# Routed results reach X by accumulating DMAs from POOL instead of loads and POOL adds

## What is computed

```python
x = x + 0.5 * _L0_ffn_ref(_layernorm(x), ...)
x = x + _L0_attn_ref(_layernorm(x), ...)
x = x + 0.5 * _L0_ffn_ref(_layernorm(x), ...)
# _L0_ffn_ref: 0.5 * shared experts + 0.5 * (each token's two best of 8 experts, weighted)
# _L0_attn_ref, per sequence of 256 tokens:
#   q, k, v = split(rms_norm(x) @ w_qkv); q, k = rms_norm(q), rms_norm(k); w = exp(k)
#   y = sigmoid(q) * cumsum(w * v) / (cumsum(w) + 1e-6)
#   u, g = split(y @ w_swiglu); x + (u * silu(g)) @ w_out
```

## Time and profile before

| what | value |
|---|---|
| runs (us) | 766.91, 769.57, 769.66; median 769.57 |
| profiled execution (us) | 770.35; its span, first to last instruction, 768.6 |
| busy share of the span | PE 89%, DVE 59%, POOL 54%, ACT 44% |
| chain that ended last | PE 68%, DVE 20%, ACT 3%, issue 3%, POOL 2%, DMA 2% |
| first add of results on POOL | 335.59 us |
| last write of attention to X | 455.46 us |
| DMA issued by POOL | 284, all indirect; 18.78 MB on its queue |

### The profile page before, as it was taken

The page is one execution under the profiler, slowest core; times in us unless marked ns, Lnnn a source line. Parts: engine busy times, 40 slices in busy tenths (PEclk is TensorE's granted clock), DMA queues, the critical chain, the costliest instruction groups (busy, mean ns, idle before and its releaser), DMA issues.

```text
span 768.6 us, 12871 instructions
## 1 busy us (share of the span) xinstructions
PE 686.6 (89%) x4282; PEld 583.7 (76%) x4282; DVE 453.1 (59%) x1137; ACT 336.7 (44%) x833; POOL 418.4 (54%) x491
## 2 busy tenths in 40 slices
PE   3879849999999999976887777999999999999995
PEld 3667738888888888953664575788888888888883
DVE  6678874444444444447999986884444444444435
ACT  2658412444444444416664526662444444444430
POOL 5600484476676665369997515006367666765330
PEclk9989959999999999999999997999999999999999
DMA  9450011111121111031100000502011112112037
GB/s 311 192 96 16 2 24 34 32 49 46 46 53 46 46 46 42 22 114 54 43 29 1 1 1 24 89 1 50 22 50 49 46 46 52 46 46 42 29 105 247
DMA packets 34782, 43.97 MB, mean 57 GB/s; under 512 B 5984, under 2 KB 27488, under 8 KB 34336
## 3 DMA queue, kind: packets, MB, share of 16 engines
q1 hardware_dynamic: 25632, 24.39, 11.2%
q0 software_dynamic: 9088, 18.78, 9.6%
HBM read 27.47 MB, written 15.66 MB: 56 GB/s over the span
## 4 chain that ended last, share of the span: by engine, by line
PE 68%; DVE 20%; ACT 3%; issue 3%; POOL 2%; DMA 2%; SPq 1%; POOLq 0%; DVEq 0%; ACTq 0%
PE psY L1466 16%; PE psH L1449 8%; PE psG L1307 6%; PE psU L1307 5%; PE psU L1309 5%; PE psG L1309 5%; PE psU L1308 5%; PE psG L1308 5%; PE psH L1378 5%; DVE rec L1063 3%; PE psT L1406 2%; DVE XN L736 2%; DVE hs L746 2%; DVE ln_stats L723 1%; DVE xn L1047 1%
## 5 line engine op out<-in xcount | busy, mean ns | idle before, releaser
L942 DVE SCALAR_TENSOR_TENSOR hr<-silu,gate,psU 128x512 f32<-128x512 f32 x142 | 106.2, 748 | 165.4 <-PE psU L1309 165.4
L639 POOL DMA_INDIRECT results<-yout,target x142 | 139.7, 984 | 114.9 <-DVE yout L968 78.9
L624 POOL DMA_INDIRECT rows<-tokens,source x142 | 137.3, 967 | 101.8 <-DVE source L898 43.5
L1214 ACT ACTIVATE silu<-psG 128x512 f32<-128x512 f32 x142 | 85.0, 598 | 162.6 <-PE psG L1309 162.4
L1466 PE MATMUL psY<-W,hT 128*128 x1120 | 148.0, 275 | 0.0
L1466 PEld LDWEIGHTS psY<-W,hT 128*128 128x128 f32 x1120 | 136.1, 192 | 0.0
L1207 ACT ACTIVATE hT<-psH 128x512 f32<-128x512 f32 x142 | 84.8, 597 | 75.9 <-PE psH L1449 75.9
L1449 PE MATMUL psH<-ident,hr 128*128 128x128 f32 x568 | 85.0, 272 | 0.0
L1449 PEld LDWEIGHTS psH<-ident,hr 128*128 128x128 f32 x568 | 70.6, 140 | 18.6
L1142 ACT ACTIVATE silu<-psG 128x512 f32<-128x512 f32 x64 | 37.9, 594 | 81.7 <-PE psG L1309 61.7
L746 DVE TENSOR_TENSOR hs<-silu,psU 128x512 f32<-128x512 f32 x64 | 43.7, 685 | 46.0 <-PE psU L1309 38.1
(11 more groups left out here) (190 smaller groups left out, 1252.2 us busy)
## 6 DMA issues: line engine op xcount, KB each, us to landing
W<-w_e SPq DMA_DIRECT2D x3, 2048.0 KB, 13.5
tokens<-XN SPq DMA_DIRECT2D x16, 260.0 KB, 6.2
Y<-results SPq DMA_DIRECT2D x32, 128.0 KB, 2.2
YF<-results SPq DMA_DIRECT2D x16, 256.0 KB, 5.8
rows<-tokens,source POOLq DMA_INDIRECT x142, 2.6
results<-yout,target POOLq DMA_INDIRECT x142, 2.3
X<-x SPq DMA_DIRECT2D x8, 256.0 KB, 5.4
out<-X SPq DMA_DIRECT2D x8, 256.0 KB, 2.8
```

Of the source, the lines that this page charges most:

```text
L624: pool.indirect_dma_start(rows[:, g % RING, t, :], None, tokens, bass.IndirectOffsetOnAxis(ap=source[:, tile:tile + 1], axis=0))\
L639: pool.indirect_dma_start(results, bass.IndirectOffsetOnAxis(ap=target[:, tile:tile + 1], axis=0), yout[:, g % 2, t, :], None).then_inc(y_ ...
L942: dve.scalar_tensor_tensor(hr[:, s.u % 2, :], silu[:, s.u % 2, :], gate[:, s.over(GT) % 2, s.u % GT:s.u % GT + 1], psU[:, s.u % 2, :], ALU ...
L1214: act.activation(silu[:, s.u % 2, :], psG[:, s.u % 2, :], ACT.Silu).then_inc(silu_done, 1)
```

## The change

SP no longer loads `Y`, and POOL no longer adds it. POOL issues DMAs that read `results` and add them to X in SBUF (`accum_op=ADD`). `ADDED` cuts X in ten pieces: four of 2 tiles (128 KB for each k), then six of 4 tiles (256 KB). For each piece the DMA for k = 0 comes first, and the one for k = 1 waits until it has landed. Six are issued ahead of the pipeline (`ADD_FIRST`), the other 14 in steps 1 to 7 as POOL's last work of the step (`ADD_STEPS`): 3, 2, 2, 2, 2, 2, 1. `at_statistics` waits for both DMAs of its batch's piece.

All depths of all four engines fall by two, as the stage of depth 1 with POOL's adds and a step of distance behind it are gone; `TURNED_STEP` and `SCORED_STEP` fall by two with them. `LN_STEPS` is worked out from the depths and the number of batches, and gives 16: (0, 1), 17: 2, 18: 3, 19: 4, 20: 5, 21: 6 where it gave 16: (0, 1), 17: 2, 18: 3, 19: 4, 21: 5, 23: 6.

```diff
-POOL_STAGES = [("qkv_rsqrt", 5), ("residual", 5), ("at_rsqrt", 3), ("mean_square", 4), ("add_routed", 1)]
-DVE_STAGES = [("at_normalise", 4), ("at_aggregate", 3), ("gate_g", 8), ("at_statistics", 2), ("gate_u", 8),
...
+POOL_STAGES = [("qkv_rsqrt", 3), ("residual", 3), ("at_rsqrt", 1), ("mean_square", 2),
+               ("add_more", 0)]
+DVE_STAGES = [("at_normalise", 2), ("at_aggregate", 1), ("gate_g", 6), ("at_statistics", 0), ("gate_u", 6),
...
+ADDED = ((0, 2), (2, 2), (4, 2), (6, 2)) + tuple((first, 4) for first in range(8, TILES, 4))
+ADD_FIRST = ((0, 0), (1, 0), (0, 1), (1, 1), (2, 0), (3, 0))
+ADD_STEPS = {1: ((2, 1), (3, 1), (4, 0)), 2: ((4, 1), (5, 0)), 3: ((5, 1), (6, 0)), 4: ((6, 1), (7, 0)),
+             5: ((7, 1), (8, 0)), 6: ((8, 1), (9, 0)), 7: ((9, 1),)}
...
-TURNED_STEP = {20: (0, 1), 21: (2,), 22: (3,), 23: (4,), 24: (5,)}
-SCORED_STEP = {21: (0,), 22: (1, 2), 23: (3,), 24: (4,)}
+TURNED_STEP = {18: (0, 1), 19: (2,), 20: (3,), 21: (4,), 22: (5,)}
+SCORED_STEP = {19: (0,), 20: (1, 2), 21: (3,), 22: (4,)}
...
-            def add_routed(s):
...
-                pool.tensor_tensor(xs, xs, Y[:, s.u % 4, 0, :, :], ALU.add).then_inc(add_link, 1)
-                wait_apart(pool, add_link, s.i + 1)
-                pool.tensor_tensor(xs, xs, Y[:, s.u % 4, 1, :, :], ALU.add).then_inc(routed_added, 1)
+            def add_results(n, k):
+
+                first, count = ADDED[n]
+                tiles = slice(first, first + count)
+                if k == 0:
+                    pool.wait_ge(sh_added, FRONT[0] if first + count <= FRONT[0] * CH else CHUNKS)
+                else:
+                    pool.wait_ge(y_added[n], 16)
+                pool.dma_start(X[:, tiles, :], results_v[:, k, tiles, :], accum_op=ALU.add).then_inc(y_added[n], 16)
...
                 if l == 0:
+                    for p in range(2):
+                        pool.wait_ge(y_sent[p], sent(0, p, GROUPS // 2))
+                    for n, k in ADD_FIRST:
+                        add_results(n, k)
+
+                    def add_more(s):
+                        for n, k in ADD_STEPS.get(s.i, ()):
+                            add_results(n, k)
...
                 def at_statistics(s):
-                    dve.wait_ge(routed_added, s.i + 1)
+                    dve.wait_ge(y_added[max(n for n, (first, _) in enumerate(ADDED) if first <= s.i * TB)],
+                                16 * TOPK)
```

More of the change, by code:

```diff
@@ L64 @@
 SUM_LAG = 1
-POOL_STAGES = [("qkv_rsqrt", 5), ("residual", 5), ("at_rsqrt", 3), ("mean_square", 4), ("add_routed", 1)]
-DVE_STAGES = [("at_normalise", 4), ("at_aggregate", 3), ("gate_g", 8), ("at_statistics", 2), ("gate_u", 8),
[L69 to L73, removed]
+POOL_STAGES = [("qkv_rsqrt", 3), ("residual", 3), ("at_rsqrt", 1), ("mean_square", 2),
+               ("add_more", 0)]
+DVE_STAGES = [("at_normalise", 2), ("at_aggregate", 1), ("gate_g", 6), ("at_statistics", 0), ("gate_u", 6),
+              ("invert", 4), ("scale_q", 4), ("weigh_v", 3), ("attend", 4), ("add_attention", 7)]
+ACT_STAGES = [("tanh_g", 6), ("denominator", 4), ("copy_yT", 5), ("copy_anT", 2), ("weights", 3), ("squares", 2)]
+PE_STAGES = [("cumulate", 4), ("transpose_y", 5), ("project", 7), ("transpose_xn", 2), ("qkv", 2),
+             ("swiglu", 5)]
+ADDED = ((0, 2), (2, 2), (4, 2), (6, 2)) + tuple((first, 4) for first in range(8, TILES, 4))
+ADD_FIRST = ((0, 0), (1, 0), (0, 1), (1, 1), (2, 0), (3, 0))
+ADD_STEPS = {1: ((2, 1), (3, 1), (4, 0)), 2: ((4, 1), (5, 0)), 3: ((5, 1), (6, 0)), 4: ((6, 1), (7, 0)),
+             5: ((7, 1), (8, 0)), 6: ((8, 1), (9, 0)), 7: ((9, 1),)}
 LN_STEPS = {}
@@ L288, in macaron @@
         memory = overlaid(
-            [("Y", [P, 4, TOPK, TB, D], fp32), ("XNT", [P, NT], fp32)],
+            [("lead", [P, 8 * TB * D], fp32), ("XNT", [P, NT], fp32)],
             [("hs", [P, 2, FT, CH * P], fp32),
@@ L296, in macaron @@
              ("silu", [P, 2, F], fp32)])
-        Y = memory["Y"]
         XNT = memory["XNT"]
@@ L401, in macaron @@
         y_sent = [sem(f"y_sent{p}") for p in range(2)]
-        y_in = [sem(f"y_in{p}") for p in range(4)]
+        y_added = [sem(f"y_added{n}") for n in range(len(ADDED))]
         yf_in = [sem(f"yf_in{c}") for c in range(CHUNKS)]
-        add_link = sem("add_link")
         last_link = sem("last_link")
@@ L409, in macaron @@
         last_added_sums = sem("last_added_sums")
-        routed_added = sem("routed_added")
         half_added = sem("half_added")
@@ L504, in _ @@
                 pipelined(sp, [(keep_tokens, 0)], CHUNKS, 2)
+                if l == 0:
+                    continue
                 for p in range(2):
                     sp.wait_ge(y_sent[p], sent(l, p, GROUPS // 2))
[L509 to L529, removed]
-                    for k in range(TOPK):
-                        sp.dma_start(Y[:, s.u % 4, k, :, :], results_v[:, k, bass.ds(s.i * TB, TB), :])\
-                          .then_inc(y_in[s.u % 4], 16)
-                pipelined(sp, [(load_results, 0)], BATCHES, 4, straight=True)
+                for c in range(CHUNKS):
+                    chunk = slice(c * CH, (c + 1) * CH)
+                    for k in range(TOPK):
+                        sp.dma_start(YF[:, k, chunk, :], results_v[:, k, chunk, :]).then_inc(yf_in[c], 16)
+                by_pe, by_dve = 0, 0
+                for c in range(CHUNKS):
+                    if c in PE_CHUNKS:
+                        by_pe += 1
+                        sp.wait_ge(last_added_sums, by_pe)
+                    else:
+                        by_dve += 1
+                        sp.wait_ge(last_added, by_dve)
+                    chunk = slice(c * CH, (c + 1) * CH)
+                    sp.dma_start(out_v[:, chunk, :], X[:, chunk, :]).then_inc(out_sent, 16)
+                sp.wait_ge(out_sent, 16 * CHUNKS)
         @block.gpsimd
@@ L691, in _, with between @@
                 if l == 0:
-                    stages = {"qkv_rsqrt": qkv_rsqrt, "add_routed": add_routed, "residual": residual,
+                    for p in range(2):
[5 more added lines that the diff above has]
+                            add_results(n, k)
+                    stages = {"qkv_rsqrt": qkv_rsqrt, "residual": residual, "add_more": add_more,
                               "at_rsqrt": at_rsqrt, "mean_square": mean_square}
-                    def scale_ahead(chunks):
+                    def between(step):
                         def run():
-                            for c in chunks:
-                                scale_ln(1, Step.of(c, 2))
+                            if step < POOL_END:
+                                for c in LN_STEPS.get(step, ()):
+                                    scale_ln(1, Step.of(c, 2))
                         return run
                     pipelined(pool, [(stages[n], d) for n, d in POOL_STAGES], BATCHES, 4, straight=True,
-                              at={k: scale_ahead(chunks) for k, chunks in LN_STEPS.items() if k < POOL_END})
+                              at={k: between(k) for k in range(POOL_END)})
         @block.vector
```

## The result

The changed kernel takes 775.32 us in the median of five runs (773.63 to 777.07), the kernel before 769.57: ratio 1.0083, with a 95% interval of 1.0059 to 1.0107. It is **slower by 0.8%**. The forecast was 771.7 (764 to 779) with 0.29 for slower; the time lies in the range, but the case that I held likeliest, no difference, did not come. The profiled execution of after took 777.07 us, its span is 775.4, 6.8 above the span of before.

What follows compares the result with a forecast made beforehand. Attention was taken as bound by POOL while filling, DVE in the middle, and PE and DVE while draining. Terms of 5.4, -0.7 and -2.6 summed to +2.1 us, a median of 771.7 us, range 764 to 779.

Steps and rivals of the forecast that it cites:

- Two steps less deep: Layer 0 attention pipeline: the two removed steps lay beside other work, so losing them saves nothing.
- rival (d): Pipeline depth: the two removed steps were real time, 10.8 us saved, 758.8 us; chance 0.03.
- What comes to POOL: POOL in attention: 20 accumulating DMAs, 1.28 us an issue (0.44 to 1.77), landing 2.3 us (2.2 to 3.4).
- The front: Before the first at_ms: issues on POOL delay it from 346.58 to 349.2 us, +2.6.
- Steps 3 to 6: Attention's fill: POOL takes 6.4 us a step against 5.4 because of two issues each, +4.0 over four steps.
- The middle: DVE-bound steps of attention: DVE needs 5.3 us a step instead of 5.42 with POOL's adds gone, -0.7.
- The drain: End of attention: layer 1's later LN work fills DVE's idle stretches, all but 0.5 of 3.1 us gained, -2.6.
- The sum: Whole kernel: +5.4 up to the DVE-bound steps, -0.7 and -2.6 after, +2.1 us in all, median 771.7.
- (b): POOL's issues: each accumulating DMA holds POOL above 1.37 us, kernel slower, 773.4 to 781.2 us; chance 0.20.
- (a): POOL's issues: each accumulating DMA costs below 0.87 us, kernel faster, 763.3 to 765.7 us; chance 0.25.
- (c): Steps with issues: DVE's normalisation and POOL block each other, up to 0.60 us a step, +3.6, 775.3; chance 0.09.

Runs made afterwards that it cites:

- the DMAs two steps apart: Changed kernel with each second-result DMA issued two steps behind its first-result DMA: 769.98 us, ratio 1.0018 to the kernel before.
- the execution with the even clock: The changed kernel run and profiled once more, nothing altered: 775.23 us, ratio 1.0095 to the kernel before.
- the larger pieces: Changed kernel with 16 accumulating DMAs in place of 20, last pieces 512 KB, in another order: 767.35 us, ratio 0.9993 to the kernel before.

## Why the prediction came out as it did

**"Two steps less deep: nothing by itself."** No run changes the depth alone, but it is bounded: without DMAs and without adds the whole kernel gains 0.54%, 4.4 us by medians, with the LN work's later place in it; rival (d) wanted 10.8 for the depth alone.

**"What comes to POOL."** This is the step that failed, twice and in opposite directions. The issue was taken from the scatter, with 0.30 of idle before each, as 1.28 us; two direct issues follow each other without the idle, and one costs 0.92. The landing was taken from the scatter as 2.3 us, with 3.4 as the far end; 256 KB landed after 4.8, beyond both ends. The rows at hand had no transfer of 256 KB on POOL's queue and none that adds, and I bounded the sizes by 128 rows of a scatter. The trace of before did have 256 KB read from `results`, on SP's queue in layer 1, and its landing lies far beyond my 3.4 (KB each, median us to landing):

```profile
YF<-results SPq DMA_DIRECT2D x16, 256.0 KB, 5.8
```

What this left out of the sum is a wait in each step: POOL has 3.87 us of other work between the issue of a piece's first DMA and its second, too little to cover that landing.

**"The front", +2.6.** Measured +4.0 by the first at_fac, 350.88 for before's

```profile
346.86 1.33 POOL L688 TENSOR_TENSOR at_fac<-at_ms,minus_half 128x6 f32<-128x6 f32 x1
```

and +5.2 counted from the start. The issues are cheaper than I had them; four waits for landings, 1.58, 0.48, 1.20 and 2.62 us in the rows of POOL above, more than make up for that.

**"Steps 3 to 6", +4.0.** Four steps from 349.94 to 375.52 took 25.58 us; the forecast said 25.6. The number is right and the reason is wrong: some 3.8 of other work, 1.83 for the pair, and 0.64 to 0.98 of waiting for the landing, where I had 2.56 of issues and no wait. Who looked at the pitch of 6.4 us alone would have taken the step for right. Two things tell the composition: the idle in brackets and the source of the issues. And the wrong reason fails at the end of the stretch: in step 7 I let one issue go and POOL be in time, but the last k = 1 DMA waited 1.33 us at 381.33. So the reciprocal of step 8 is 7.0 late and that of step 9 7.8 (388.28 for 380.52 before), not 5.4; from the start 8.2 and 9.0.

**"The middle", -0.7.** From step 9 to 13 21.48 us, before 21.78: 0.07 a step instead of 0.12. The normalisation does take 0.60 us now instead of 0.8 to 0.9, but the pitch is 5.39 with and without DMAs. Part of the saving goes to a new short wait: wkv starts 0.44 us behind ysc (395.37 to 395.81), before 0.34 (387.77 to 388.11), just after ACT's tq has ended at 395.78. Four steps at 0.12 would have given 0.5; 0.3 came.

**"The drain", -2.6.** Mechanism right. The traces say 1.8; the runs, 1.8 to 2.9, don't exclude the 2.6. I let 0.5 of the 3.1 us of idle stay; 1.34 stays, before the last addition, where PE's psY ends last, and LN work on DVE can't shorten PE's chain.

**The sum** forecast +2.1 for 5.4 - 0.7 - 2.6. By the execution with the even clock it is 7.15 at step 13 and -1.66 behind it, +5.5 at the last addition; counted from the start 8.5 and 6.8. The medians of the runs differ by 5.75, and by 6.5 the second time. That the time came out slower, as summed, is luck: two errors went against each other. By the forecast's own points (3.85 us faster with an issue of 0.87 us, 2.4 faster with one of 0.97) the measured 0.92 would have made the kernel some 3 us faster, an estimate; the 10.5 us of waits, for which the sum had next to nothing, turned that round.

**The rivals.** The time lies in the span of (b), but (b)'s mechanism did not happen: the issue was cheaper than I forecast, not dearer. (a) asked for an issue below 0.87 us; it was near that, 0.85 to 0.95, and still the kernel was slower, so the list lacked the rival that came true: a landing longer than the work that stands behind its issue, for which an in-order engine has to wait. The text had the wait ("each first result") and priced it at a landing of 2.3. (c) is not seen: with the DMAs two steps apart the pairs at 346.58, 352.18 and 357.97 lie beside a normalisation and take 1.82 to 1.83 us, as those of the changed kernel do that lie beside none. The Trainium skill's page "SBUF — State Buffer", section "Who interferes with whom", says that DVE in a two-port mode and GpSimd shut each other out for a whole instruction, whoever comes second, and that a DMA stalls so when GpSimd lacks port time for its descriptors. These rows show no such stall; which mode the normalisation runs in, no run here shows.

**What beats both kernels** is the kernel before with the LN work two steps later: 0.9976 (0.9962 to 0.9990). The accumulating DMAs in their best order tried are level with the kernel before, 0.9993, but they have the LN work late as well; POOL's adds with the LN work late are at 0.9976. So no run shows a gain from replacing the adds. Taking them off POOL for nothing gives 0.54% with the LN work late, by the ratios 0.3% more than that place alone.

**What stays open**: why the runs of the larger pieces gain 0.07% and not the 0.24% of before with LN late, though attention takes as long in the two traces (the intervals overlap); and what makes the clock fall in the drain of some executions. PE was busy for 1.56 of the 4 us ahead of the fall, but for 2.01 where none followed. The kernel without DMAs had 1.88 and kept its clock; the one with plain DMAs had 1.87 and lost it.

## What to carry to other kernels

A pitch that comes out as forecast doesn't show that its parts did: look at the idle in brackets and at who waited. When an engine that works in order must wait for its own transfer, price the landing against the work that stands between issue and wait, and put a step more between them than the median needs; here that alone was worth 5 us. Marks of two traces are compared from where the changed stretch begins, not from the start of the span: here 1.5 us of a lead was made ahead of it. And before pricing a replacement, run the kernel with neither the old work nor the new: the floor, 0.54%, says how much there is to win.

## What the hardware showed that I had not expected

- An accumulating DMA costs more than a plain one at both ends: its issue on POOL 0.95 us against 0.55 in the median (0.92 against 0.57 in a pair), its landing 4.8 against 3.2 us for 256 KB (3.2 against 2.4 for 128 KB), and the DMA engines 6.8 against 3.2 us for a MB.
- The issue hardly depends on the size, 0.85 to 0.87 us for a single one of 128 KB, 0.92 to 0.95 for 256 and 512 KB; the landing does, 3.6, 4.7 and 6.7 us in one kernel.
